# Row maxima of the first head group taken and turned by halves of the queries, with gates and bias computed earlier

## What is computed

```python
h = _layernorm(x, axis=-1) * (1 + ca) + sa
x = x + ga * _L0_attn_ref(h, ...)          # 16 heads of 16 features
h = _layernorm(x, axis=-1) * (1 + cb) + sb
x = x + gb * _L0_ffn_ref(h, ...)           # squared relu, spike count
```

```python
sc = jnp.where(causal, scores.reshape(b, h, nb, WIN, nb, WIN), NEG_INF)
m = jnp.max(sc, axis=-1, keepdims=True)
e = jnp.exp(sc - jnp.where(jnp.isfinite(m), m, 0.0))
probs = e / jnp.where(denom == 0.0, 1.0, denom)     # per window
attn_probs = jax.nn.softmax(probs.reshape(b, h, s, s), axis=-1)
```

## Time and profile before

| | before |
|---|---|
| median of 3 runs | 2437.61 us (2433.52 to 2437.72) |
| the profiled execution | 2435.94 us |
| its span in the profile | 2434.2 us |
| TensorE busy | 2239.7 us (92%) |
| VectorE busy | 1717.2 us (71%) |
| ScalarE busy | 1544.4 us (63%) |
| GpSimd busy | 1199.1 us (49%) |

### The profile page before, as it was taken

The page is one execution under the profiler, slowest core; times in us unless marked ns, Lnnn a source line. Parts: engine busy times, 40 slices in busy tenths (PEclk is TensorE's granted clock), DMA queues, the critical chain, the costliest instruction groups (busy, mean ns, idle before and its releaser), DMA issues.

```text
span 2434.2 us, 46643 instructions
## 1 busy us (share of the span) xinstructions
PE 2239.7 (92%) x19196; PEld 1245.9 (51%) x19196; DVE 1717.2 (71%) x2034; ACT 1544.4 (63%) x2162; POOL 1199.1 (49%) x1120
## 2 busy tenths in 40 slices
PE   6788889999999999999999999999999999989857
PEld 4344334455545555465554555455554655445446
DVE  5677887778677676877777677876768766785412
ACT  2376676766667667666667666676667666667511
POOL 3143123535754457634765456544566256434654
PEclk8799999999999999999999999999999999999979
DMA  6222112311122113211223111121133101110000
GB/s 201 76 81 81 46 53 66 94 47 30 54 66 81 51 34 88 74 52 30 57 64 105 47 37 58 55 81 51 34 88 87 32 20 45 49 29 8 16 20 18
DMA packets 113808, 140.21 MB, mean 58 GB/s; under 512 B 8456, under 2 KB 86440, under 8 KB 113600
## 3 DMA queue, kind: packets, MB, share of 16 engines
q1 hardware_dynamic: 113600, 137.23, 19.8%
HBM read 74.26 MB, written 58.74 MB: 55 GB/s over the span
## 4 chain that ended last, share of the span: by engine, by line
PE 76%; DVE 10%; POOL 6%; ACT 5%; issue 2%; DMA 1%; SPq 0%; POOLq 0%; ACTq 0%; DVEq 0%
PE pv L672 10%; PE sums L662 9%; PE score L647 9%; PE ring L625 9%; PE sums L608 8%; PE score L596 8%; PE score L564 5%; PE score L547 5%; DVE e L996 4%; PE ring L703 4%; DVE negmax L979 3%; ACT e L868 2%; PE ring L628 2%; POOL below L1232 2%; PE score L650 2%
## 5 line engine op out<-in xcount | busy, mean ns | idle before, releaser
L868 ACT ACTIVATE e<-score 128x512 f32<-128x512 f32 x1152 | 672.1, 595 | 392.7 <-PE score L650 213.8
L996 DVE TENSOR_TENSOR e<-ring,e 128x1024 f32<-128x1024 f32 x576 | 680.1, 1222 | 289.5 <-PE ring L703 288.5
L979 DVE TENSOR_REDUCE negmax<-ring 128x8 f32<-128x1024 f32 x512 | 606.3, 1219 | 134.7 <-PE ring L628 131.1
L873 ACT ACTIVATE e<-e 128x2048 f32<-128x2048 f32 x288 | 548.5, 1905 | 2.3 <-DVE e L996 2.3
L647 PE MATMUL score<-q_st,k_st 112*128 112x512 bf16 (+3 forms) x1536 | 459.4, 330 | 61.8 <-ACT e L868 22.5
L625 PE MATMUL ring<-k_st,q_st 96*128 96x512 bf16 (+3 forms) x1536 | 381.6, 333 | 42.7 <-DVE e L996 18.5
L1241 POOL TENSOR_SCALAR r_p<-r_b,ab 128x256 bf16<-128x256 f32 x96 | 90.2, 940 | 560.9 <-DVE r_b L1002 520.7
L672 PE MATMUL pv<-e,v 128*17 128x512 f32 (+3 forms) x3072 | 313.4, 496 | 0.0
L1220 POOL TENSOR_TENSOR gT<-gT 128x512 f32<-128x512 f32 x128 | 135.5, 1063 | 359.1 <-ACT gT L847 359.1
L608 PE MATMUL sums<-w_proj,gT 128*128 128x256 f32 x1024 | 294.9, 398 | 17.4 <-ACT n L854 8.8
L662 PE MATMUL sums<-e,d_ones 128*32 128x256 f32 x4608 | 304.4, 382 | 2.0 <-ACT e L868 0.7
(11 more groups left out here) (133 smaller groups left out, 2620.1 us busy)
## 6 DMA issues: line engine op xcount, KB each, us to landing
q_st<-q_parts SPq DMA_DIRECT2D x31, 768.0 KB, 6.0
k_st<-k_parts SPq DMA_DIRECT2D x31, 768.0 KB, 8.6
q_parts<-qk_p SPq DMA_DIRECT2D x30, 384.0 KB, 2.5
k_parts<-qk_p SPq DMA_DIRECT2D x28, 384.0 KB, 2.6
x_in<-in_x SPq DMA_DIRECT2D x8, 1024.0 KB, 5.8
x_res<-in_x SPq DMA_DIRECT2D x32, 256.0 KB, 4.2
out<-acc SPq DMA_DIRECT2D x32, 256.0 KB, 2.2
q_parts<-qk_p SPq DMA_DIRECT2D x30, 256.0 KB, 2.9
```

Of the source, the lines that this page charges most:

```text
L868: act.activation(e[:, n % ES, hh, :], score[SCORE_SLOT["st", n, hh][0]][:, :], ACT.Exp, scale=DK ** -0.5).then_inc(e1_done, 1)
L873: act.activation(v, v, ACT.Exp).then_inc(e2_done, 1)
L979: dve.tensor_reduce(negmax[:, hh, 8 * t:8 * t + 8], slot[:, :].rearrange("p (a n) -> p a n", n=P), AX_X, ALU.max, negate=True).then_inc(ri ...
L996: dve.tensor_tensor(v, ring[no % 2][:, :].rearrange("p (i n) -> p i n", i=2), v, ALU.mult).then_inc(ring_free, 1)
```

## The change

`TILES` is a new packing of the same 36 windows per head into again 18 tiles. Its entries now say which windows of a block stand in a tile, so that block 4 can be cut into three parts. The first five tiles (`FIRST_TILES`) hold the blocks 0 to 3, that is the first half of the queries of all four heads. The places of the maxima (`SLOT_OF`, `SLOTS`) are renumbered so that each half is one stretch. The number of reduces per group stays 18, that of masks 32. The number of score matmuls per group goes from 48 to 52 with the same columns in total.

For group 0 only, `BEGIN_TILES` tiles (13) are taken before step 0, three more in step 0 and two in step 1 (`BEGIN_AT`). The first half is split after tile 5 and turned behind tile 7. The second half is split after the 18th tile and turned at the end of step 1 (`late_turn`), since unit 2 is the first to need it. The 18 tiles of group 1 move from steps 1 to 6 to steps 2 to 7 (`SECOND_AT`), and its turn from step 7 to step 8 (`SECOND_TURN`). From group 2 on the steps have three tiles each as before, in the new packing.

The landing of the maxima is now waited for head by head, and the first stacks are loaded with one head per transfer, in eight transfers. On TensorE the bias, the gates and the columns now stand behind QK 3, ahead of QK 4.

```diff
-TILES = []
-for _p in range(2):
-    for _hh in (2 * _p, 2 * _p + 1):
-        TILES += [[(_hh, 7, 0)], [(_hh, 6, 0), (_hh, 0, 896)], [(_hh, 5, 0), (_hh, 1, 768)], [(_hh, 4, 0), (_hh, 2, 640)]]
-    TILES.append([(2 * _p, 3, 0), (2 * _p + 1, 3, 512)])
-SLOTS = 40
-SLOT_OF = {7: 0, 6: 8, 0: 15, 5: 16, 1: 22, 4: 24, 2: 29, 3: 32}
-TILES_AT = {1: [0, 1, 2], 2: [3, 4, 5], 3: [6, 7, 8], 4: [9, 10, 11], 5: [12, 13, 14], 6: [15, 16, 17]}
+TILES = [[(_h, 0, 0, 1), (_h, 2, 0, 3), (_h, 3, 0, 4)] for _h in range(QH)]
+TILES.append([(_h, 1, 0, 2) for _h in range(QH)])
+FIRST_TILES = len(TILES)
+for _h in range(QH):
+    TILES += [[(_h, 7, 0, 8)], [(_h, 4, 4, 1), (_h, 6, 0, 7)], [(_h, 5, 0, 6), (_h, 4, 0, 2)]]
+TILES.append([(_h, 4, 2, 2) for _h in range(QH)])
+
+SLOT_OF = {5: 0, 4: 6, 6: 11, 7: 18, 0: 26, 2: 27, 3: 30, 1: 34}
+HALF_SLOTS = [(26, 42), (0, 26)]
+SLOTS = 42
+
+TILES_AT = {1: 3, 2: 3, 3: 3, 4: 3, 5: 3, 6: 3}
 TURN_AT = 7
+BEGIN_TILES = 13
+BEGIN_AT = {0: 3, 1: 2}
+SECOND_AT = {2: 3, 3: 3, 4: 3, 5: 3, 6: 3, 7: 3}
+SECOND_TURN = 8
...
+def late_turn(n):
+
+    return n == max(BEGIN_AT)
...
-            for pair in range(2):
+            for hh in range(QH):
                 for stacked, dram in ((q_st, part_dram[0]), (k_st, part_dram[1])):
-                    sp.dma_start(stacked[0:KROWS, 0, 2 * pair:2 * pair + 2, :],
-                                 dram[0, 2 * DK * pair:2 * DK * pair + 2 * DK, :, :].rearrange("(h d) a n -> (d a) h n", h=2)).then_inc(first_stack[pair], 16)
+                    sp.dma_start(stacked[0:KROWS, 0, hh, :],
+                                 dram[0, DK * hh:DK * hh + DK, :, :].rearrange("d a n -> (d a) n")).then_inc(first_stack[hh], 16)
...
-                if u == 0:
-                    pe.wait_ge(m_in, 16 * QH * (g + 1))
+                if u == 0 and g:
+                    pe.wait_ge(m_in[hh], 16 * g)
+                elif g == 0 and u in (0, MIXED):
+                    pe.wait_ge(first_m_in[int(u == MIXED)][hh], 16)
...
-            for item in PROLOGUE[4:]:
+            for item in PROLOGUE[4:8]:
                 piece(item)
...
-            for k in range(len(TILES)):
-                if k == 1:
-                    pe.wait_ge(cols_ready, 2)
+            for item in PROLOGUE[8:]:
+                piece(item)
+            pe.wait_ge(cols_ready, 2)
+            for k in range(BEGIN_TILES):
                 maxima(0, k)
-            turn_maxima(0)
+                if k == FIRST_TILES + 1:
+                    turn_maxima(0, range(NB // 2))
...
+                if late_turn(n):
+                    turn_maxima(*turns(n))
...
+                if g == 0 and k == FIRST_TILES - 1:
+                    split_maxima(g, k, range(NB // 2))
+                elif k == len(TILES) - 1:
+                    split_maxima(g, k, range(0 if g else NB // 2, NB))
```

More of the change, by code:

```diff
@@ L153, in tiles_of @@
 def tiles_of(n):
-    g = n // NU + 1
-    return [(g, k) for k in TILES_AT.get(n % NU, ())] if 0 <= n < NUNIT and g < NG else []
+    g, s = n // NU + 1, n % NU
+    if not 0 <= n < NUNIT:
+        return []
+    out = []
+    if n in BEGIN_AT:
+        at = BEGIN_TILES + sum(BEGIN_AT[k] for k in BEGIN_AT if k < n)
+        out += [(0, k) for k in range(at, at + BEGIN_AT[n])]
+    table = SECOND_AT if g == 1 else TILES_AT
+    if g < NG and s in table:
+        at = sum(table[k] for k in table if k < s)
+        out += [(g, k) for k in range(at, at + table[s])]
+    return out
 def turned_out(n):
@@ L165 @@
 RING_NO = {}
-for _k in range(len(TILES)):
+for _k in range(BEGIN_TILES):
     RING_NO["m", 0, _k] = len(RING_NO)
@@ L178, in turns, with turn_of, turn_no @@
 def turns(n):
-    g = n // NU + 1
-    return g if n % NU == TURN_AT and 0 <= n < NUNIT and g < NG else None
+    g, s = divmod(n, NU)
+    if late_turn(n):
+        return 0, range(NB // 2, NB)
+    if 0 <= n < NUNIT and g + 1 < NG and s == (TURN_AT if g else SECOND_TURN):
+        return g + 1, range(NB)
+    return None
+def turn_of(g, blocks):
+    return g, int(g == 0 and blocks[0] > 0)
+def turn_no(g, blocks):
+    return 1 + g if blocks[0] == 0 and g else turn_of(g, blocks)[1]
+def late_turn(n):
+    return n == max(BEGIN_AT)
 def mixed(n):
@@ L195, in score_slots @@
         st = [("st", n, hh) for hh in range(QH)] if n < NUNIT else [None] * QH
-        turn = ("turn", turns(n), 0) if turns(n) is not None else None
+        turn = ("turn", *turn_of(*turns(n))) if turns(n) else None
         begin = [p[0], st[0]] if mixed(n) else [st[0], p[0]]
-        steps.append([*begin, st[1], turn, st[2], st[3], p[1]])
+        steps.append([*begin, st[1], st[2], st[3], p[1], turn] if late_turn(n) else [*begin, st[1], turn, st[2], st[3], p[1]])
     for order in steps:
@@ L629, in maxima, with turn_maxima @@
                         c = stop
+                    off = end
                 mm.then_inc(ring_ready, 1)
[L632 to L635, removed]
+            def turn_maxima(g, blocks):
+                view = score_bank("turn", *turn_of(g, blocks)).bitcast(BF16)
+                pe.wait_ge(max_lo, turn_no(g, blocks) + 1)
+                for i in blocks:
                     at = SLOT_OF[i]
@@ L772, in step @@
                     scores(n, 1)
-                if turns(n) is not None:
-                    turn_maxima(turns(n))
+                if turns(n) and not late_turn(n):
+                    turn_maxima(*turns(n))
                 if 0 in at:
@@ L854, in take_sum, with take_turned @@
                 act.activation(n1[:, D * i:D * i + D], sums[:, HALF:HALF + D], ACT.Copy, scale=-1.0).then_inc(back_evac, 1)
-            def take_turned(g):
-                if g:
-                    act.wait_ge(m_in, 16 * QH * g)
-                act.wait_ge(turn_ready, g + 1)
-                act.copy(m_sb[0:QH * MROWS, :], score[SCORE_SLOT["turn", g, 0][0]][:, :].bitcast(BF16)[0:QH * MROWS, :]).then_inc(turned, 1)
+            def take_turned(g, blocks):
+                for hh in range(QH):
+                    if g == 1:
+                        act.wait_ge(first_m_in[0][hh], 16)
+                        act.wait_ge(first_m_in[1][hh], 16)
+                    elif g:
+                        act.wait_ge(m_in[hh], 16 * (g - 1))
+                act.wait_ge(turn_ready, turn_no(g, blocks) + 1)
+                own = slice(P * blocks[0], P * blocks[-1] + P)
+                act.copy(m_sb[0:QH * MROWS, own],
+                         score[SCORE_SLOT[("turn", *turn_of(g, blocks))][0]][:, :].bitcast(BF16)[0:QH * MROWS, own]).then_inc(turned, 1)
             def first_exp(n, hh):
@@ L921, in step @@
                     first_exp(n, 1)
-                if turns(n) is not None:
-                    take_turned(turns(n))
+                if turns(n) and not late_turn(n):
+                    take_turned(*turns(n))
                 for item in sums_ended(n, 1):
```

81 lines of the change are left out of this document (41 added, 40 removed).

## The result

The changed kernel takes 2428.57 us (median of 7 runs, 2425.18 to 2429.53) against 2437.61 (7 runs, 2433.08 to 2438.33): 9.0 us less by the medians. The ratio estimated from all these runs is 0.9965, 95% interval 0.9954 to 0.9977, or 0.35% faster. The profiled execution took 2428.17 us with a span of 2426.4, beside 2435.94 and 2434.2 before.

What follows compares the result with a forecast made beforehand. TensorE bounds the long middle and step 0, VectorE steps 1 to 6. Start gains 19.5 - 4.7 - 1.9 - 2.5 = 10.4 us, packing loses 1.9: 8.5 off 2437.6 gives 2429, own range 2425 to 2433, with rivals 2423 to 2437.

Steps and rivals of the forecast that it cites:

- Gates and bias: Before the tiles: placed behind QK 3, they let the first reduce start at 46.2 us instead of 51.1, saving 4.9.
- Step 0: Start of group 0: with the first half turned early, step 0 begins at 62.2 us instead of 81.7, 19.5 earlier.
- stuck in the queue: First half's maxima wait in the DMA queue for weights until 69.5 us; step 0 about 70.5, time 2437; chance 0.08.
- Steps 0 and 1: Scores of step 0 to those of step 2: 4.7 us given back to the second turn, leaving a lead of 14.8.
- The clock: At step 2: TensorE idles some 4 us ahead of it, then a stretch of 5 us at 1.2 GHz costs 2.5.
- Group 1 to step 9: Steps 2 to 9, with group 1's reduces, split and turn: 1.9 us of lead lost.
- The packing: New tiles in the 31 later groups: 0.06 us lost per group, 1.9 us in all.
- The rivals at 0.2 and more a group: Later groups: packing costs 0.2 us (2433) or 0.3 (2436), chance 0.20; slower, 0.44 us a group, 2440.8, chance 0.07.
- The clock rival: Tiles ahead of step 0: clock stays at 2.4 GHz, `BH` takes 3 us instead of 6; gain 14.5, 2423; chance 0.15.

Runs made afterwards that it cites:

- experiment 3: The kernel before with only TensorE's bias, gates and columns moved behind QK 3, all else as it was; 2432.46 us, ratio 0.9979.
- Experiment 1: The changed kernel with both feed-forward weight loads issued behind the first half's maxima on SyncE's queue instead of ahead; 2420.65 us, ratio 0.9931 against the kernel before.
- experiment 2: The changed kernel with the old packing of tiles in all groups but the first; 2430.46 us, ratio 0.9972 against the kernel before.
- 4: The changed kernel with bias, gates and columns back behind the last projection, so the halves alone; 2431.16 us, ratio 0.9976 against the kernel before.
- 5: The changed kernel with 15 tiles ahead of step 0, three in step 0, and the second half's turn a step earlier; 2422.38 us, ratio 0.9942 against the kernel before.
- experiment 7: The changed kernel with weights issued behind the first maxima, 15 tiles ahead of step 0 and the second turn in step 0; 2419.38 us, ratio 0.9931.
- 8: The changed kernel with weights behind the first maxima, all 18 tiles ahead of step 0, second turn in step 0; 2418.26 us, ratio 0.9924.
- Kernel 6: The changed kernel with weights behind the first maxima, 15 tiles ahead of step 0, second turn there, old packing in later groups; 2422.63 us, ratio 0.9945.

## Why the prediction was right, and where it wasn't

The time, 2428.57 against 2429, and the sign were right. The sum behind it holds one large miss, which smaller ones and the scatter of the clock made up.

**Gates and bias: right.** First reduce at 46.8, forecast 46.2, and experiment 3 gives the part 5.1 us (forecast 4.9). Only the 7.4 us of VectorE's work was not: moved from 43.8 to 32.5 it took 8.7 us (32.55 to 41.25). That had room: the first reduce still waited 5.52 us for its tile.

**Step 0: the step that failed.** I had 62.2 and it was 68.0. The five reduces, the split, the transposes and tile 13 came within 0.8 us of the forecast. The order in the queue was named too, and the price of it was wrong: the term "the weights are in at 62 to 62.5" measured 67.5. I had kept before's 20.5 us from the issue of the next batch (`x_in`) to the landing of `w_proj` and moved it whole, to begin at 42. It began at 42.9 and took 24.6 us. Two parts of it grew. From the issue of `x_in` to the landing of `w_fc` it took 19.6 us instead of 17.6, while the first stacks were still moving: their last one landed at 46.35, while in before the DMA engines were idle from 46 to 48. Experiment 3 has that too (19.4), and it is the one that lands at 61.9. And from the landing of `w_fc` (62.5) to that of `w_proj` it took 5.0 us instead of 2.8 (2.7 in experiment 3). In these 5.0 us the trace has 406 packets of 2048 bytes, 0.83 MB, where before and experiment 3 have none. In the first 100 us only the loads of stacks have that size, so these are the stacks of group 1, issued at 61.0, behind the maxima, and moving beside the last of `w_proj`. That they delay it is argued from this, since no experiment held them back. Full DMA engines alone do not explain the miss, as experiment 3 shows: with a share of 1.09 in 44 to 52 us its landing moved nearly as much as its issue.

Experiment 1 shows what the order costs. `w_proj`, now issued at 58.31, behind the maxima, took 9.4 us and landed at 67.7, 0.2 later than in after for an issue 3.0 later, and the maxima landed from 59.6 to 60.2. Their 3.1 us beside such traffic are also more than the 2.0 of the earlier trace rows. The Trainium skill, in DMA: Bandwidth & Descriptors, section Queues, rings and completion order, lets each DMA engine consume one queue's descriptors in ring order. These runs agree: the same four transfers take 8.1 to 11.8 us behind the weights and 3.1 to 4.5 ahead of them. The rival "stuck in the queue" was the same mechanism with 69.5 for the landing, so the truth lay between my forecast and it, nearer to the rival.

**Steps 0 and 1: smaller than forecast.** From the scores of step 0 to those of step 2 it took 17.6 us, not 19.8. `BH` took 4.6 us instead of 6.0 or more, since the clock rose within it (granted 0.61 in 68 to 72 us, 1.00 in 72 to 76), so the first reduce behind it came 6.1 us after step 0 began and not 8.1. The scores of step 2 began at 85.65, a lead of 11.2 where 14.8 was forecast: 5.8 lost at step 0, 2.2 won back here. The wait for the landing that the change adds there was real, at 1.38 us.

**The clock: right for this execution.** From the scores of step 2 to the third sum the lead fell from 11.2 to 8.5, 2.7 us (forecast 2.5). The window that answers to the fall:

```profile
82.00:88.00 6.00, 3.73 (x33) 2.17 (x34) 1.10 (x4) 1.77 (x3) 0.00 (x0) 0.73 0.04 12
88.00:94.00 6.00, 6.00 (x46) 3.50 (x44) 4.56 (x6) 2.25 (x5) 0.00 (x0) 0.70 0.01 3
```

The size is not steady: between the same two events experiments 1, 2 and 4 lose 1.5, 1.4 and 1.7 us. The cause is shown by its absence: in experiments 5, 7 and 8, with no wait ahead of step 2, the lead falls by 0.1 between the second and the third sum.

**Group 1 to step 9: about right.** 1.4 us were lost instead of 1.9, in other places than forecast. The split ended at 127.1 and not 122, since all of it began 4 us late.

**The packing: right.** 0.057 us a group, forecast 0.06, by the trace of after, and 0.05 against experiment 2. That it is invisible in the times also follows from its size. The rivals at 0.2 and more a group are out.

**What made it up.** At the ninth sum the lead was 7.1 instead of 10.4. It then rose by 1.5 at the 17th sum, where in the profile of before the clock fell and in that of after it didn't, and by 0.9 at the 44th, where it fell in both, but before lost more. With the packing's 1.8 off and rests of a few tenths, that ends at 8.4. Nothing of the change aims at these two, and experiments 1, 4 and 8, with the same tiles as after, have the long distance from the 16th to the 17th sum again (10.1 to 10.5). I take them for how two single executions fell out, which one profile of each kernel can't show, and I had no term for it. So the profiles' 7.8 us (2435.94 to 2428.17) and the medians' 9.0 differ by less than this scatter. That my sum met the median to 0.4 us is luck in good part: with step 0 alone as measured it would have read 2434.9, and with the whole start as measured (a lead of 7.1 instead of 10.4) 2432.4.

**The clock rival** (2.4 GHz through the tiles) was wrong for the tiles. The level fell at about 51 us, 0.50 in 52 to 62. My reason against it does not hold in the same way: TensorE was busy not half of the time but 6.61 of 8.00 us in 44 to 52. In other executions it held for longer in the same stretch (0.70 in experiment 1, 0.81 in 5), so this too varies. It was partly true in `BH`.

**What stays open.** What group 1's stacks alone cost the landing, and how much of the weights' 24.6 us is due to the four further transfers of the first stacks, was not tested. Why the clock falls at a given small hole in one execution and not in the next isn't settled. Kernel 6 fell in it more often than 7 in the profiled executions, but with six runs from 2418 to 2427 nothing says that the old packing causes it.

## What to carry to other kernels

Before a step is moved earlier, look at what stands ahead of its small transfer in the same DMA queue, and price the landing of that bulk anew: it depends on when the whole train of transfers begins and on what else moves beside it, what is issued behind it too, and not only on its own issue. Issuing the small one first cost one line and gained as much again as the whole change (9.0 us, then 8). Where two halves of a chain are split to start sooner, price the second half's wait together with the clock that it takes down. Starting step 0 some 3 to 5 us later, with all tiles done, was as fast, within the intervals, as starting it as soon as it could. And where an edit is worth less than the scatter of the runs, compare it by a quantity that repeats in the trace, here the change of the lead over each batch.

## What was unexpected in the hardware

- The granted clock fell in small holes of TensorE in the middle of one execution and not at the same place of another (0.61 against 1.00 with the same 3.00 us busy in the window). The falls cost 1 to 3 us in the table of experiment 7, and the runs of one kernel lie 2 to 9 us apart.
- The same small VectorE operations took 0.41 us in one place and 1.3 to 1.4 in another: the last of the bias 0.41 before and 1.26 after the change, the first scaling of the gates 1.39 before and 0.41 after. In both kernels GpSimd was in a run of operations of 1.2 us beside the slow ones and idle beside the fast ones. No experiment took GpSimd away, so the cause is argued only.
- Two transfers of weights, issues of 0.7 and 0.6 us on SyncE, added 5 to 7 us to each of four small transfers behind them.
- A transfer that is issued later can move its data first: 0.83 MB of the stacks of group 1 moved between 62.5 and 67.5 us, before the maxima that were issued ahead of them had landed (67.8 to 68.5). That this slowed the landing is argued only.
